# Attention memory: rates as rows of 8 batches, scanned there and spread over the partitions by transfers

## The reference, cut to what matters

```python
alpha = (sigmoid(hidden @ aW.T + ab) * 0.1).mean(-1)
eta   = (sigmoid(hidden @ eW.T + eb) * 0.9 + 0.05).mean(-1)
theta = (softplus(hidden @ tW.T + tb) * 0.1).mean(-1)
# g: gradient of |silu(k W1^T) W2^T - v|^2 at each token, with the weights at the chunk's start, clipped by norm
def step(S, W):                       # one token t
    S = eta[t] * S - theta[t] * g[t]
    W = (1 - alpha[t]) * W + S
    return S, W
out[t] = silu(q[t] @ W1[t].T) @ W2[t].T
```

## Time and profile before

| | us |
|---|---|
| median of 3 runs | 760.18 |
| profiled execution | 759.91 |
| its span, first to last instruction | 757.8 |
| TensorE busy in the span | 657.4 |
| VectorE busy | 596.8 |
| ScalarE busy | 446.7 |
| POOL busy | 250.0 |

### The profile page before, as it was taken

How to read it: one execution, slowest core, us unless ns; L and a number is a source line. 1 busy time by engine, 2 the same in 40 slices (tenths; PEclk the granted TensorE clock), 3 DMA queues, 4 the chain that set the end, 5 groups by cost and what they waited for, 6 DMA issues and landing times. The chain is left out here.

```text
span 757.8 us, 15078 instructions
## 1 busy us (share of the span) xinstructions
PE 657.4 (87%) x5491; PEld 566.2 (75%) x5491; DVE 596.8 (79%) x1373; ACT 446.7 (59%) x1126; POOL 250.0 (33%) x201
## 2 busy tenths in 40 slices
PE   5449999998687889999999999999988469999996
PEld 2138989897576778878787797878867257989985
DVE  0878877862498999999899998997975869887851
ACT  1516566661466777678786777877453456657550
POOL 0033462214211445151542607243151051651302
PEclk9859999999899999999999999999999669999999
DMA  8959726340501014031130401303012714753401
GB/s 337 422 181 365 261 94 234 128 126 29 174 1 56 1 32 137 1 112 58 56 112 1 155 15 56 112 2 112 1 57 73 261 49 144 258 171 144 138 8 35
DMA packets 58225, 89.23 MB, mean 118 GB/s; under 512 B 6961, under 2 KB 49073, under 8 KB 58033
## 3 DMA queue, kind: packets, MB, share of 16 engines
q1 hardware_dynamic: 46176, 70.28, 26.6%
q0 software_dynamic: 3840, 10.49, 4.2%
q10 hardware_dynamic: 8144, 7.61, 3.2%
HBM read 74.73 MB, written 22.02 MB: 128 GB/s over the span
## 5 line engine op out<-in xcount | busy, mean ns | idle before, releaser
L726 PE MATMUL ps<-moe_normedT_high,weights_high_up 128*128 128x320 f32 x252 | 80.9, 321 | 0.9 <-DVE moe_hidden_low L544 0.8
L727 PE MATMUL ps<-moe_normedT_low,weights_high_up 128*128 128x320 f32 x252 | 78.2, 310 | 0.0
L728 PE MATMUL ps<-moe_normedT_high,weights_low_up 128*128 128x320 f32 x252 | 78.2, 310 | 0.0
L726 PE MATMUL ps<-weights_high_down,moe_hidden_high 128*128 128x256 f32 x256 | 73.4, 287 | 0.0
L544 DVE SCALAR_TENSOR_TENSOR moe_hidden_low<-ps,moe_hidden_high 128x256 fp32r<-128x256 f32 x128 | 54.1, 422 | 22.7 <-ACT moe_hidden_high L681 18.6
L728 PE MATMUL ps<-weights_high_down,moe_hidden_low 128*128 128x256 f32 x256 | 71.6, 280 | 0.0
L727 PE MATMUL ps<-weights_low_down,moe_hidden_high 128*128 128x256 f32 x256 | 71.5, 279 | 0.0
L1194 POOL TENSOR_TENSOR weights_raw_up<-weights_raw_up,att_AB 128x1024 f32<-128x1024 f32 x8 | 18.9, 2358 | 139.9 <-DVE att_AB L1401 139.9
L640 ACT CAST weights_high_down<-weights_raw_down 128x256 fp32r<-128x256 f32 x96 | 35.0, 406 | 39.2 <-PE ps L728 39.2
L726 PEld LDWEIGHTS ps<-weights_high_down,moe_hidden_high 128*128 128x128 f32 x256 | 48.0, 188 | 3.1 <-issue 3.1
L318 DVE TENSOR_TENSOR weights_low_down<-weights_raw_down,weights_high_down 128x256 fp32r<-128x256 f32 x128 | 50.0, 418 | 0.0
(11 more groups left out here) (329 smaller groups left out, 2037.0 us busy)
## 6 DMA issues: line engine op xcount, KB each, us to landing
weights_raw_up<-in_w SPq DMA_DIRECT2D x16, 1024.0 KB, 8.8
weights_raw_down<-in_w SPq DMA_DIRECT2D x16, 1024.0 KB, 8.3
first_xt<-in_xT SPq DMA_DIRECT2D x8, 1024.0 KB, 7.8
weights_rows<-x SPq DMA_DIRECT2D x8, 1024.0 KB, 5.4
out_x<-weights_rows SPq DMA_DIRECT2D x8, 1024.0 KB, 4.6
weights_rows<-x ACTq DMA_DIRECT2D x7, 1024.0 KB, 5.4
weights_rows<-x SPq DMA_DIRECT2D x2, 512.0 KB, 4.3
weights_raw_up<-in_w_x SPq DMA_DIRECT2D x1, 768.0 KB
```

Source lines behind the costliest of these rows:

```text
L726: mm(dst, high_l, high_r, start=start, stop=False)
L727: mm(dst, high_l, low_r, start=False, stop=False)
L728: return mm(dst, low_l, high_r, start=False, stop=stop)
```

## The change

The means of alpha and eta are no longer repeated on all partitions by TensorE. Eight small products, each with a window of a matrix that has 1/64 in two columns, put the mean of alpha of sequence b in row b and of eta in row 32 + b. ScalarE reads the two blocks of 8 x 128 into `rates`. On these 8 partitions VectorE scans the running products (`decay`, `gain`, `mixed`). SP stores the rates to memory and reads them back with every one of the 128 partitions reading the same row, into `eta` and `keep`; it does the same with the decays, into `AB`, whose 129th column takes what `carry` gave to `mix`. Column 0 of each sequence is cleared in memory once. The scans of carry and AB over 128 partitions go, and with them `carry` and `lead`. The second scores' product moves ahead of the last key tap, and the momentum scan follows gate 0 and that tap. The readers of AB wait for its transfers.

```diff
-    carry = sb("carry", [P, B, CH])
+    rates, zeros = sb("rates", [B, 2, CH]), sb("zeros", [B, CH + 1])
+    decay, mixed, gain = sb("decay", [B, CH]), sb("mixed", [B, CH + 1]), sb("gain", [B, CH])
     theta_log = sb("theta_log", [P, B, D])
     theta_sum = sb("theta_sum", [P, B])
-    lead, idents = sb("lead", [P, B, CH]), sb("idents", [P, B, CH])
+    idents = sb("idents", [P, B, CH])
 
...
-    P1, M, AB = sb("P1", [P, B, CH]), sb("M", [P, B, CH]), sb("AB", [P, B, CH])
+    P1, M, AB_ends = sb("P1", [P, B, CH]), sb("M", [P, B, CH]), sb("AB", [P, B, CH + 1])
+    AB = AB_ends[:, :, 0:CH]
+    rates_dram = nc.dram_tensor("rates_row", (2, B, CH), F32, kind="Internal").ap()
+    decays_dram = nc.dram_tensor("decays_row", (2, B, CH + 1), F32, kind="Internal").ap()
...
+            def over_rows(row, rows):
+                return bc(row.rearrange("b t -> (b t)").unsqueeze(0), [rows, row.shape[0] * row.shape[1]])
+
+            def spread_rates(c):
+                sp.wait_ge(rates_read, 2 * c + 2)
+                if c:
+                    sp.wait_ge(keep_loaded, 16 * c)
+                    sp.wait_ge(eta_loaded, 16 * c)
+                sp.dma_start(rates_dram[:, :, 1:].rearrange("i b t -> b i t"), rates[:, :, 1:]).then_inc(rates_stored, 16)
+                sp.wait_ge(rates_stored, 16 * c + 16)
+                if c:
+                    sp.wait_ge(mom_ready, c)
+                    sp.wait_ge(m_ready, c)
+                for i, dst, done in (1, eta, eta_loaded), (0, keep, keep_loaded):
+                    sp.dma_start(dst[:].rearrange("p b t -> p (b t)"), over_rows(rates_dram[i], P)).then_inc(done, 16)
+
+            def spread_decays(c):
+                sp.wait_ge(decays_made, 4 * c + 4)
+                if c:
+                    sp.wait_ge(ab_loaded, 64 * c)
+                sp.dma_start(decays_dram[0, :, 0:CH], decay[:]).then_inc(decays_stored, 16)
+                sp.dma_start(decays_dram[1], mixed[:]).then_inc(decays_stored, 16)
+                sp.wait_ge(decays_stored, 32 * c + 32)
+                if c:
+                    sp.wait_ge(hid2_ab_ready, c)
+                    sp.wait_ge(qab_ready, c)
+                    sp.wait_ge(mix_ready, 2 * c)
+                for n, own, other in SIDES:
+                    for i, rows in (0, own), (1, other):
+                        sp.dma_start(AB_ends[rows, n, :].rearrange("p b t -> p (b t)"), over_rows(decays_dram[i, n, :], D)
+                                     ).then_inc(ab_loaded, 16)
+
             load_res(0)
+            sp.wait_ge(cleared, 1)
+            sp.dma_start(rates_dram[0, :, 0:CH], zeros[:, 0:CH]).then_inc(rates_cleared, 16)
+            sp.dma_start(rates_dram[1, :, 0:CH], zeros[:, 0:CH]).then_inc(rates_cleared, 16)
+            sp.dma_start(decays_dram[0], zeros[:]).then_inc(rates_cleared, 16)
+            sp.wait_ge(rates_cleared, 48)
...
+            for c in range(2):
+                spread_rates(c)
+                spread_decays(c)
             for c in range(NCH - 1):
                 sp.wait_ge(x2_ready, 2 * c + 2)
                 store(c)
                 sp.wait_ge(x2_stored, 16 * c + 16)
                 sp.wait_ge(x2_turned, 2 * c + 2)
                 load_res(c + 1)
+                if c + 2 < NCH:
+                    spread_rates(c + 2)
+                    spread_decays(c + 2)
...
             def query_decay(c, very_first):
-                pool.wait_ge(ab_ready, c + 1)
+                pool.wait_ge(ab_loaded, 64 * c + 64)
...
-                pool.wait_ge(ab_ready, c + 1)
+                pool.wait_ge(ab_loaded, 64 * c + 64)
...
                     g.tensor_tensor(MIX[:, n, other], bc((fold_low if own is UPPER else fold_high)[:].unsqueeze(1), [P, HALF, D]),
-                                    bc(carry[:, n, CH - 1:CH], [P, HALF, D]), ALU.mult).then_inc(mix_ready, 1)
+                                    bc(AB_ends[:, n, CH:CH + 1], [P, HALF, D]), ALU.mult).then_inc(mix_ready, 1)
...
             def start():
-                v.memset(lead[:], 0.0).then_inc(folded, 1)
-                v.memset(eta[:, :, 0:1], 0.0)
-                v.memset(keep[:, :, 0:1], 0.0).then_inc(folded, 1)
+                v.memset(zeros[:], 0.0).then_inc(cleared, 1)
...
             def momentum_scans(c):
-                dve.wait_ge(eta_ready, c + 1)
-                dve.wait_ge(folded, 7)
+                dve.wait_ge(eta_loaded, 16 * c + 16)
+                dve.wait_ge(folded, 5)
                 v.tensor_tensor_scan(run(mom[:]), run(eta[:]), run(idents[:]), 0.0, ALU.mult,
                                      ALU.add).then_inc(mom_ready, 1)
 
-            def carry_scans(c, first):
-                if not first:
-                    dve.wait_ge(mix_ready, 2 * c)
-                for n, _, other in SIDES:
-                    last = v.tensor_tensor_scan(run(carry[other, n, :]), run(eta[other, n, :]), run(lead[other, n, :]),
-                                                0.0, ALU.mult, ALU.add)
-                last.then_inc(carry_ready, 1)
+            def decay_scans(c):
+                dve.wait_ge(rates_read, 2 * c + 2)
+                if c:
+                    dve.wait_ge(decays_stored, 32 * c)
+                v.tensor_tensor_scan(gain[:], rates[:, 1, :], zeros[:, 0:CH], 1.0, ALU.mult, ALU.add).then_inc(decays_made, 1)
+                v.tensor_tensor_scan(decay[:], rates[:, 0, :], zeros[:, 0:CH], 1.0, ALU.mult, ALU.add).then_inc(decays_made, 1)
+                dve.wait_ge(decays_made, 4 * c + 1)
+                v.tensor_tensor_scan(mixed[:, 0:CH], rates[:, 0, :], gain[:], 0.0, ALU.mult, ALU.add).then_inc(decays_made, 1)
+                v.tensor_copy(mixed[:, CH:CH + 1], gain[:, CH - 1:CH]).then_inc(decays_made, 1)
 
...
             def memory_scans(c, very_first):
-                dve.wait_ge(keep_ready, c + 1)
+                dve.wait_ge(keep_loaded, 16 * c + 16)
...
-            def decay_scans(c, first):
-                dve.wait_ge(carry_ready, c + 1)
-                if not first:
-                    dve.wait_ge(qab_ready, c)
-                v.tensor_tensor_scan(run(AB[:]), run(keep[:]), run(carry[:]), 0.0, ALU.mult,
-                                     ALU.add).then_inc(ab_ready, 1)
...
             def decayed_hidden(c):
                 dve.wait_ge(hid2_ready, c + 1)
                 dve.wait_ge(hid2_doubled, c + 1)
-                v.tensor_tensor(hid2_ab[:], hid2[:], AB[:], ALU.mult).then_inc(hid2_ab_ready, 1)
+                dve.wait_ge(ab_loaded, 64 * c + 64)
+                v.tensor_tensor(hid2_ab[:], hid2[:], AB, ALU.mult).then_inc(hid2_ab_ready, 1)
...
                 if first:
-                    carry_scans(c, True)
-                    decay_scans(c, True)
-                if first:
                     stats_of(c + 2)
                 convolve_queries(c + 1)
+                decay_scans(c + 1)
                 key_taps(c + 1, 1 - par, range(1, 2))
                 decayed_hidden(c)
-                key_taps(c + 1, 1 - par, range(2, TAPS))
-                if first:
-                    second_scores(c, par)
+                key_taps(c + 1, 1 - par, range(2, 3))
+                second_scores(c, par)
+                key_taps(c + 1, 1 - par, range(3, TAPS))
                 gates(c + 1, 1 - par, (0,), first)
                 momentum_scans(c + 1)
-                if not first:
-                    second_scores(c, par)
-                carry_scans(c + 1, False)
                 gates(c + 1, 1 - par, (1,), first)
                 memory_scans(c + 1, False)
                 ends(c + 1, 1 - par, first)
-                decay_scans(c + 1, False)
                 gates(c + 1, 1 - par, (2, 3), first)
...
             convolve_queries(0)
+            decay_scans(0)
             gates(0, 0, (0, 1), True, True)
             momentum_scans(0)
             gates(0, 0, (2, 3), True, True)
...
-            def keep_rates(c, first):
-                src = DD if first else BB
-                act.wait_ge(rates_made, 2 * c + 1)
-                if not first:
-                    act.wait_ge(ab_ready, c)
-                for n, own, _ in SIDES:
-                    s.activation(carry[own, n, 0:1], wide(src)[own, n, 0:1], ACT.Copy, bias=0.95, scale=-0.05)
-                s.activation(keep[:, :, 1:], wide(src)[:, :, 1:], ACT.Copy, bias=0.95, scale=-0.05).then_inc(keep_ready, 1)
-
-            def momentum_rates(c):
-                act.wait_ge(rates_made, 2 * c + 2)
-                for n, _, other in SIDES:
-                    s.activation(lead[other, n, 0:1], wide(A)[other, n, 0:1], ACT.Copy, bias=0.5, scale=0.45)
-                s.activation(eta[:, :, 1:], wide(A)[:, :, 1:], ACT.Copy, bias=0.5, scale=0.45).then_inc(eta_ready, 1)
+            def mean_rates(c):
+                act.wait_ge(rates_made, c + 1)
+                if c:
+                    act.wait_ge(rates_stored, 16 * c)
+                    act.wait_ge(decays_made, 4 * c)
```

(44 more changed lines are left out.)

21 lines of the change are left out of this document (12 added, 9 removed).

## The result

| | before, us | changed, us |
|---|---|---|
| median (20 runs each, on one chip) | 760.25 | 756.51 |
| lowest to highest | 758.74 to 762.52 | 753.44 to 763.90 |
| profiled execution | 759.91 | 756.85 |
| its span | 757.8 | 754.9 |
| TensorE busy | 657.4 | 655.8 |

The changed kernel takes 0.9948 of the time of the one before (95% interval 0.9929 to 0.9967): 3.9 us less by that ratio and 3.7 by the medians, where 11.7 were forecast (the sum itself gave 11.2). It is faster, outside my range (741 to 753), and its runs spread over 10.5 us where those of before spread over 3.8.

The account below looks back on a forecast made before the run. TensorE and VectorE were both taken as full in a 45.6 us step; 2.8 us in the first chunks plus 6 x 1.4 gave 11.2 us off the 760.2 median, 749.0, stated as 748.5; range 741 to 753.

Parts of the forecast that it names:

- the sum itself: Whole kernel: 2.8 us from the first chunks plus 6 steps of 1.4 us, 11.2 us less.
- the rival of a slower kernel by the round trip: Momentum scan waits for eta's transfer through memory: 1.7 us a step worse over 6 steps, 770 us; chance 0.06.
- the hold: POOL's decayed queries beside VectorE's memory scan delay gate 2: 1.4 us a step gained in place of 2.1; chance 0.50.
- VectorE's lead: Ahead of the keys' turn: VectorE 1.15 us ahead of what TensorE needs, if no scan is held.
- the rates' products: TensorE's eight products of 128 columns take 1.0 us instead of 1.92: 0.9 us less a step.
- the first chunks: Chunk 0 and step 0: 3.9 us gained net of 1.5 for decay scans, 2.8 with the momentum scan pushed 1.1.
- a touch by a mix product: POOL's mix product delays VectorE's gate 2 from 408.85 to 409.05.
- POOL spoils more: Taps, momentum and end copies each wait once for POOL: 0 to 0.8 us a step, 752 to 759; shared chance 0.11.
- a sign of being wrong: Rates' products on TensorE taking 1.9 us would show the forecast wrong; 1.0 was expected.

Follow-up runs that it names:

- e1: Changed kernel with POOL's decayed queries waiting until the end copies are made: 764.01 us, 0.9805 of the kernel before, step 43.79 us.
- e9: Changed kernel with POOL's decayed queries behind the end copies and the last key tap ahead of the second scores' product: 742.32 us, 0.9757 of the kernel before.
- e2: Changed kernel with the last key tap back ahead of the second scores' product: 765.50 us, 0.9841 of the kernel before, step 43.97 us.
- e11: Changed kernel with only POOL's wait for the end copies added, run again on another set's chip: 743.69 us, 0.9763 of the kernel before.
- e5: The changed kernel again, unaltered, as partner of later runs on one chip: 774.32 us, 0.9966 of the kernel before; profiled run's steps 47.1 us.
- e6: Changed kernel with the second scores' product back behind the momentum scan (step 0: behind the taps): 768.95 us, 0.9897 of the kernel before.
- e12: Changed kernel with POOL waiting for the end copies and the second scores' product back behind the momentum scan: 748.94 us, 0.9838 of the kernel before.
- e10: Changed kernel with POOL's wait, last tap ahead of the product, and step 0's decayed queries and mix before the gradient's norm, repeated: 744.34 us, 0.9783 of before.
- e3: Kernel before with one edit, the second scores' product ahead of the last key tap: 806.90 us, 1.0367 of the kernel before.
- e8: Changed kernel with POOL's wait, last tap ahead of the product, and step 0's decayed queries and mix before the gradient's norm: 761.73 us, 0.9792 of before.

## Why the prediction was wrong

**The bound and the order of events: right in the main.** AB was to land near 402.4, and its landing woke POOL at 402.32. The queries were then to wait for the momentum scan until 403.1; in this step that scan was over at 402.00 and they began at once, in others they waited for it (3.70 us in place of 2.18). The memory scan was to last some 3.9 us: 4.03 here, 3.50 in four of six steps. The decay scans were to take 0.43 each: 0.39 to 0.40. Eta and keep were to be hidden: VectorE stood for none of the new transfers, so the rival of a slower kernel by the round trip falls. The step that failed is what the hold costs, together with VectorE's lead against it; two smaller terms of the sum were off as well, the rates' products and the first chunks.

**The hold (0.7 forecast, 1.7 measured).** I forecast 1.4 us a step with it and 2.1 without. Without it, e1 gains 45.65 - 43.79 = 1.9, near the 2.1. With it, 0.2. The forecast's 0.7 was 1.65 of scan and 0.2 of "a touch by a mix product", less VectorE's lead of 1.15. The scan's part was right: 1.76 in the step shown, 1.23 in four others. The touch was 0.7: the first two mix products held an end copy each, 0.25 and 0.43 us longer than plain. That makes 2.44. And the lead was 0.5, not 1.15, which e1 shows, where nothing is held: VectorE's third gate addition starts at 411.20 and TensorE's keys' turn, which follows such an addition's start by 0.96 us when it waits for it (407.66 and 408.62 above), starts at 412.69, 0.53 later than it could. 2.44 - 0.53 = 1.91, and the step shown is 45.73 - 43.79 = 1.94 longer than e1's. In the four others 1.23 + 0.68 - 0.53 = 1.38, and they are 1.4 longer (45.2), but for the first of them, whose 45.50 stand against 44.36 in e1. So the rival "POOL spoils more", priced at 752 to 759 and given 0.11 together with another, is what happened. The row on which I had sized it shows one held operation; beside five POOL operations in a row several of VectorE's were held, each anew: one or two scans and two copies a step. The Trainium skill ("SBUF — State Buffer", section "Who interferes with whom") names two kinds of VectorE work that the shared port pair can hold: two SBUF inputs, and copies and tensor-with-scalar operations where they run in a mode that uses both ports. The trace agrees with the first by the scan (4.03 us against 2.28), and the end copies (0.41 and 0.59 against 0.17) fit the second, though no run shows in which mode they ran; I had weighed only the first.

**VectorE's lead (1.15 forecast, 0.5 measured): the product's new place.** The forecast let VectorE take up the product 0.35 us after it was free. It stood 1.76 us for TensorE's scores (396.31): VectorE was early, with 1.0 us of decay scans and copy instead of 1.45, and TensorE late, 0.7 of it because its rates had saved less. The last tap, 1.5 us of work that could have filled that time, stood behind the product. With the tap ahead (e9) the same gate addition starts at 397.99 and the keys' turn at 400.83, a lead of 1.9; there a hold of 2.4 would cost 0.5 and one of 1.9 nothing, and e2, which has the tap ahead and POOL's hold, takes 43.97 against 43.78.

**The rates' products (0.9 forecast, 0.2 measured).** I took 1.0 us from eight products over half the rows "since the weights are narrow". Eight of 128 columns over all rows, 1.95 in the earlier trace rows, were the nearer ones: against 1.92 before, 0.2 less leaves 1.7, and their row in the timeline shows 1.83, close to the 1.9 that I had named as a sign of being wrong.

Without the hold, the waits of TensorE that went are 0.34 and 0.86 as forecast, and with 0.2 for the rates that is 1.4 of the 1.9. The remaining 0.5 us, which the forecast did not have, made up for most of what the rates did not save. Three stretches of TensorE's list, ahead of L2158, L2136 and L2030, are 0.13 to 0.15 us shorter each in e9 besides the waits; why, I have not traced. That the gain without the hold came near 2.1 is in so far luck.

**The first chunks (2.8 forecast, 1.6 measured).** The 2.8 had in it 1.5 us of loss for chunk 0's decay scans, which lie ahead of the first att_P. They took 1.0, and step 0 gained 47.54 - 44.97 = 2.6, so the sum is 1.6. Step 0 alone was to gain 4.3 with the hold and 5.4 without. Without it e1 takes 41.87 us there, a gain of 5.7: the three waits of the earlier trace rows, 4.5 us, are gone, as forecast. Of the 3.1 us between 44.97 and 41.87, some 1.6 are TensorE's clock behind the longer wait in chunk 0, which I had not thought of, and the other 1.5 are left for the hold, where I had 1.1: POOL's work for chunk 1 starts in that step at 264.10, ahead of both wide scans.

**What stays open.** Why TensorE's clock falls behind a wait in one execution and not behind the same wait in another: a step 0 of 41.87 or of 45.55 us in one kernel (e1, e11) goes with it, and in e5 a mean step of 47.1 in place of 45.5. With e1's wait the runs spread over 4 us (e1, 5 runs) and 6 (e11, 6 runs) instead of 10 (20 runs) and 17 (12 runs); from so few runs this can't be called a difference. And e6 and e12 have the same steps, but 0.9897 and 0.9838 of the kernel before, each on another chip; their profiled executions, from which the steps are, stand at 0.9885 and 0.9879.

## What to carry to other kernels

When a transfer replaces computed data, look not only at whether it lands in time but at which engine wakes on its landing, and beside whose two-input work: here POOL's operations had some 4 us to spare and could wait for VectorE's scans to be over, and that one added wait made the change worth 2.0% (e1) to 2.4% (e11) instead of 0.5%. When two waits end near each other, test the edits in a square: here neither alone gained anything, and one of them, alone in the kernel before, cost 3.7%. An engine's lead is a quantity to be recounted after the change: whatever makes it earlier (shorter scans) moves work into a wait unless something is left to fill it.

## What the runs showed of the hardware

- Where a POOL operation that reads SBUF met a VectorE scan with two SBUF inputs, the second to start ended about its plain length after the first had ended. Scan 2.28 us, 4.03 behind the decayed queries; POOL's mix product 0.61 us, 2.61 behind the scan; the queries 2.2 us, 3.00 behind a scan.
- Small operations are held too: copies of 128 x 4, 0.17 us, took 0.41 and 0.59 beside POOL's operations, and 1.98 in a step of e2 and one of e6; in e1 all took their plain length. A 128 x 8 operation took 1.73 us in step 0 beside the decayed queries (in e1 too, where these stay in place there) and 0.17 in e10, where they are moved.
- TensorE's granted clock, at 1.00 before, fell (to 0.50 where a stretch shows the low level alone) behind waits of 3.44 and 3.58 us (e3), of 1.81, 1.97, 2.02, 2.06, 2.21 and 2.43 (e5), and of 2.44 in chunk 0 (changed, e8, e11, e12). It stayed at 1.00 behind waits of 1.22 and 1.24 (e5), of 1.73 and 2.01 (changed), and behind the same wait of 2.43 or 2.44 in chunk 0 in e1, e9 and e10.
- A fall behind the wait in chunk 0 lengthened the 4.33 us from the keys' turn to L2073 to 5.94 (changed), 5.92 (e8) and 6.90 (e11).
- Issuing AB's four transfers took SyncE 2.37 us in most steps, a median of 0.59 each; those of eta, 0.5 MB, took 0.34 to 0.36 and those of keep 0.42 to 0.90.
